# Causal maxima masked by halves of the keys, and a new order for the launch of a six-layer kernel

## The chip, the cores and the metric

One core of one Trainium2 chip. The metric is the device time in microseconds of one execution; the kernel before takes 808.35 us as the median of three runs.

## The reference, cut to what matters

Six residual layers on x of shape (4, 512, 128), each on the layer-normalised x. The change touches the first, a causal self-attention with 16 heads of 8 dimensions and rotary positions:

```
q = rope(xn @ wq + bq);  k = rope(xn @ wk + bk);  v = xn @ wv + bv
score = where(causal, q k^T / sqrt(8), -inf);  attn = softmax(score)
x = x + (attn v) @ wo + bo
```

Behind it come a cross-attention with 77 keys, a mixture of 8 experts of which each token takes 2, another self-attention, a single-head cross-attention and a convolutional feed-forward layer.

## The kernel before

Instructions are written for each engine in an order of its own, and semaphores tie them together. The 512 tokens of each of the 4 batches lie as 4 tiles of 128 partitions. An attention layer is cut into 16 units: unit g works on batch g // 4 and on 4 of the 16 heads. A0 is the causal layer, X0 the cross-attention, A1 the second self-attention. The units of A0 and X0 are one stream, those of A1 another.

**Maxima.** The softmax takes the true maximum of each row, so a unit computes its scores twice. First with queries as output partitions (`max_pe`, L574), from which VectorE reduces the negated maximum along the keys (`max_dve`, L590); GpSimd splits it in two bf16 parts (`neg_of`), TensorE turns them (`turn_pe`, L611) and a DMA puts them as further rows into the unit's stack. Then with keys as output partitions (`scores_pe`, L690), from which ScalarE takes the exponential (L715), GpSimd masks the diagonal block (L723) and TensorE multiplies with the values (`pv_pe`, L738). Each head's operands are split into bf16 parts, stacked along 64 rows, so two heads lie side by side in the array as rows 0 to 63 and 64 to 127 and can run at once. The maxima of a unit are 12 items, each one bank of up to 512 columns, with 16 diagonal blocks in all. To a diagonal block two more matmuls add -1e30 above the diagonal (`pair_q` with `behind_pair`, L578, and `even_q` with `behind_even`, L579), each with 64 rows, 128 weight columns and 128 streamed columns. Units 0 and 1 have their maxima ahead of the stream; those of unit g + 2 run between the scores of unit g.

**Launch.** Before unit 0 each batch goes through these steps. VectorE takes the moments of its rows (`moments_dve`, L450), GpSimd the inverse root (`norm_pool`, L477), VectorE normalises (L471), TensorE transposes (`norm_pe`, L528), ScalarE copies to `xnT` (`norm_act`, L542). TensorE projects q, q with neighbours swapped, k, k swapped, and v (`stage0_pe`, L1233 and L1236). VectorE adds the bias and multiplies with cosine and sine (`stage0_dve`, L1244 and L1247), GpSimd adds the two products (`roped_pool`, L1261), ScalarE rounds to the first bf16 part (`stage0_act`, L1275), VectorE subtracts it (`rest0_dve`, L1255), ScalarE rounds the second part (L1280), GpSimd subtracts again for the third (`part3_pool`, L1267). The parts lie in one buffer, `parts`. SP sends them to a stack in DRAM with six DMAs per batch (`stack_dma`, L914, three for q and three for k), and loads each unit's slot from there (`load_sp`, L638 and L644). GpSimd adds the output bias to x for each batch (`bias_pool`, L823).

The order by hand: all of GpSimd's constants come first, and TensorE and VectorE wait for all of them (`s_const`, 5). TensorE then takes the transposes of batches 0 and 1, the projections of 0 and 1, transposes of 2, projections of 2, transposes of 3, projections of 3, the 12 maxima of unit 0, its turn, the 12 maxima of unit 1, and unit 0. It and VectorE wait for all weights of the layer at once. ScalarE may write `parts` of a batch only when the stack DMAs of the batch before have landed. SP issues x of batch 0, ten loads, x of batches 1 to 3, the fills, further weights, the stack of batch 0, four slot loads, and the stacks of 1, 2 and 3, with the shift of unit 0's maxima ahead of the last.

Of the kernel before, what the change touches and what calls it, by code (L numbers as in the profile page):

```python
# [12 lines left out]
BF16 = mybir.dt.bfloat16  # L13
# [3 lines left out]
P = 128  # L17
NB, S, D = 4, 512, 128
QT = S // P
# [42 lines left out]
SLOT_DMAS = 2  # L62
TURNS = 4
# [181 lines left out]
def stacked_by(a, b, z):  # L245

    if z == 0:
        return 16 * RUNS * (NB * a.order + b + 1)
    return 16 * RUNS * (b + 1 if a is A0 else NB + 1 if a is X0 else NB + 2 + b)


def build(nc, d, out):
# [4 lines left out]
    with es:  # L257
# [12 lines left out]
        s["emptied"] = [sem(f"emptied{i}") for i in range(TURNS)]  # L270
        s["slot"] = [sem(f"slot{i}") for i in range(UNITS)]
# [17 lines left out]
        pair_q, even_q = sb("pair_q", [P, 2 * P], BF16), sb("even_q", [P, 2 * P], BF16)  # L289
        behind_pair, behind_even = sb("behind_pair", [P, 2 * P], BF16), sb("behind_even", [P, 2 * P], BF16)  # L290
# [91 lines left out]

        after_w = w12[:, 4:W_PIECES].rearrange("p a n -> p (a n)")
# [22 lines left out]
        s_x0, s_x = sem("s_x0"), sem("s_x")  # L406
        s_w, s_out_w, s_soon, s_later, s_experts = [sem(f"s_{n}") for n in ("w", "out_w", "soon", "later", "experts")]
        s_padded, s_padb = sem("s_padded"), sem("s_padb")
        s_fill, s_filled0, s_filled = sem("s_fill"), sem("s_filled0"), sem("s_filled")
        s_const = sem("s_const")  # L410
# [29 lines left out]
        def moments_dve(e, ln, b):  # L440

            n = norm_number(ln, b)
            if ln == 0:
                e.wait_ge(s_x0 if b == 0 else s_x, 16)
            else:
                e.wait_ge(*x_at[(ln - 1, b)])
# [110 lines left out]
        def half(t, j):  # L557
            return t[rows_of(j), P * j:P * (j + 1)]

        def max_pe(e, g, m):  # L560
# [7 lines left out]
            for qt in tiles:  # L568
                for h in hs:
# [58 lines left out]
        def load_sp(e, g):  # L628
# [4 lines left out]
            e.wait_ge(s["stacked_q"], stacked_by(a, b, 0))  # L633
            e.wait_ge(s["stacked_k"], stacked_by(a, b, 1))
# [246 lines left out]

        def split_pool(e, a, b, z, step):
# [3 lines left out]
            if step == 0:  # L886
                e.wait_ge(*emptied(("qk"[z], a.ln, b)))
                e.wait_ge(s["stacked_k" if z else "stacked_q"],
                          stacked_by(a, b, z) - 16 * RUNS)
# [11 lines left out]

        def stack_dma(e, a, b, z):
# [7 lines left out]
            for first, rows, part, same in (K_RUNS if z else Q_RUNS):  # L910
                src = parts[:, z, part:part + (1 if same else rows), 0:n]
# [357 lines left out]
        def stage0_act(e, b):  # L1269
# [6 lines left out]
            if b in (1, 2):  # L1276
                norm_act(e, 0, b + 1)
# [1120 lines left out]
```

## Time and profile before

| | |
|---|---|
| median of 3 runs | 808.35 us (808.21 to 808.52) |
| the profiled execution | 808.57 us, span 806.8 us |
| busy in the span | TensorE 652.0 us (81%), VectorE 568.1 (70%), ScalarE 431.9 (54%), GpSimd 285.3 (35%) |
| mean granted TensorE clock | 0.905 of 2.4 GHz |
| first score of unit 0 | 73.58 us |

The span runs from the first to the last instruction; what the run takes beyond it lies around the profiled instructions. In the rows below PE is TensorE, PEld its weight loads, DVE VectorE, ACT ScalarE, POOL GpSimd and SP the queue that issues most DMAs; PEclk is the granted clock of TensorE as a share of 2.4 GHz. A busy share says how full an engine is; the chain of work that ended last says which waits set the end.

### The profile page before, as it was taken

Reading aid. Unit: us, or ns where it says so; the run is one execution under the profiler, and the core shown is the slowest. Engines: PE = TensorE matmul, PEld = TensorE weight load, DVE = VectorE, ACT = ScalarE, POOL = GpSimd, SP = SyncE. Lnnn points to the kernel's source line nnn. Section 1 sums busy time; section 2 is a strip of 40 time slices with the busy share of each in tenths; the row PEclk is TensorE's granted clock in tenths of the full one; section 3 lists DMA queues with packets and bytes.
Section 4 is the critical chain, followed back from the end, with each engine's and each line's share of the span. In section 5 each row is a group of like instructions: output and inputs, shape, how many; then the busy total and the mean of one; then the engine's idle time right before and its main releaser. Section 6 shows DMA issues by size and latency. Waiting matters only on the chain.

```text
span 806.8 us, 16037 instructions
## 1 busy us (share of the span) xinstructions
PE 652.0 (81%) x5011; PEld 354.7 (44%) x5011; DVE 568.1 (70%) x1685; ACT 431.9 (54%) x825; POOL 285.3 (35%) x517
## 2 busy tenths in 40 slices
PE   2758999999978886169999924598899989997987
PEld 1334455444434443159999812132232323334543
DVE  3757678787757776737777626888898898943564
ACT  1322555666666543035566412086787777884544
POOL 5742444454551345713333301215132241341310
PEclk9885999999999999579999956598999999999999
DMA  7452655354223311211111135201322111000000
GB/s 221 149 199 83 199 163 171 113 176 145 71 67 99 102 53 63 77 32 51 52 48 48 42 108 182 78 27 34 127 81 78 54 29 52 2 2 1 13 14 27
DMA packets 72788, 67.18 MB, mean 83 GB/s; under 512 B 14545, under 2 KB 67217, under 8 KB 72705
## 3 DMA queue, kind: packets, MB, share of 16 engines
q1 hardware_dynamic: 70000, 60.68, 24.6%
q0 software_dynamic: 2272, 4.69, 1.8%
q8 instruction: 42, 0.69, 0.4%
q10 hardware_dynamic: 432, 0.79, 0.3%
q14 instruction: 42, 0.34, 0.1%
HBM read 37.74 MB, written 28.00 MB: 81 GB/s over the span
## 4 chain that ended last, share of the span: by engine, by line
PE 60%; DVE 20%; issue 7%; POOL 5%; ACT 4%; DMA 3%; SPq 1%; DVEq 0%; ACTq 0%; POOLq 0%
PE bank_pv L738 11%; DVE mx L590 11%; PE bank_turn L574 7%; PE bank_scores L2034 5%; PE bank_turn L1768 4%; PE bank_scores L1776 4%; PE bank_scores L1768 4%; PE bank_scores L690 4%; POOL routed_tokens L1732 2%; PE bank_turn L757 2%; DVE stats L450 2%; DVE xn L471 2%; PE bank_turn L799 2%; PE bank_turn L578 2%; PE bank_turn L528 2%
## 5 line engine op out<-in xcount | busy, mean ns | idle before, releaser
L590 DVE TENSOR_REDUCE mx<-bank_turn 128x1 f32<-128x512 f32 (+3 forms) x452 | 259.6, 615 | 60.3 <-PE bank_turn L579 31.4
L574 PE MATMUL bank_turn<-stk 64*128 64x77 bf16 (+4 forms) x708 | 160.1, 303 | 30.0 <-DVE mx L590 20.0
L690 PE MATMUL bank_scores<-stk 64*128 64x512 bf16 (+3 forms) x576 | 169.4, 355 | 4.8 <-ACT probs L711 3.6
L715 ACT ACTIVATE probs<-bank_scores 128x1024 f32<-128x1024 f32 (+4 forms) x160 | 117.2, 768 | 98.6 <-PE bank_scores L690 98.3
L711 ACT ACTIVATE probs<-bank_scores 128x512 f32<-128x512 f32 x256 | 138.6, 606 | 35.6 <-PE bank_scores L690 34.6
L738 PE MATMUL bank_pv<-probs,vsl 128*32 128x512 f32 (+3 forms) x1152 | 137.6, 550 | 2.8 <-POOL probs L723 1.8
L574 PEld LDWEIGHTS bank_turn<-stk 64*128 64x128 bf16 x708 | 52.2, 96 | 133.8 <-DVE mx L590 64.5
L723 POOL TENSOR_SCALAR_AFFINE_SELECT probs<-probs 128x256 f32<-128x256 f32 x128 | 51.8, 408 | 73.6 <-ACT probs L715 72.2
L1748 POOL DMA_INDIRECT expert_outputs<-probs,y_at x39 | 37.3, 957 | 83.2 <-DVE y_at L1645 78.8
L477 POOL TENSOR_TENSOR rstd<-var,mhalf 128x4 f32<-128x4 f32 x24 | 25.4, 1056 | 108.4 <-DVE var L456 108.2
L690 PEld LDWEIGHTS bank_scores<-stk 64*128 64x128 bf16 x576 | 45.6, 93 | 29.4 <-ACT probs L711 17.5
L528 PE MATMUL bank_turn<-ident,xn 128*128 128x128 f32 x60 | 13.0, 354 | 56.2 <-DVE xn L471 56.0
L579 PE MATMUL bank_turn<-behind_even,even_q 64*128 64x128 bf16 x256 | 53.1, 229 | 0.0
L578 PE MATMUL bank_turn<-behind_pair,pair_q 64*128 64x128 bf16 x256 | 53.0, 229 | 0.0
L2034 PE MATMUL bank_scores<-f_w1c,w 128*128 128x512 f32 x96 | 47.5, 634 | 0.4 <-ACT w L537 0.4
L604 POOL CAST neg<-mx 128x16 bf16<-128x16 f32 x33 | 6.5, 196 | 112.6 <-DVE mx L590 99.4
L590 DVE TENSOR_REDUCE mx<-bank_scores 128x1 f32<-128x512 f32 x60 | 40.8, 680 | 3.0 <-PE bank_scores L574 3.0
L1776 PE MATMUL bank_scores<-w,oT 128*128 x312 | 41.4, 276 | 1.3 <-DVE probs L1665 1.0
L1768 PE MATMUL bank_turn<-probs,w_now 128*128 128x128 f32 x320 | 42.2, 280 | 0.0
L542 ACT COPY xnT<-bank_turn 128x512 f32<-128x512 f32 x19 | 11.1, 583 | 55.8 <-PE bank_turn L528 55.8
L1768 PEld LDWEIGHTS bank_turn<-probs,w_now 128*128 128x128 f32 x320 | 40.1, 197 | 0.0
L1768 PE MATMUL bank_scores<-probs,w_now 128*128 128x128 f32 x304 | 39.1, 275 | 0.0
(303 smaller groups left out, 1163.0 us busy)
## 6 DMA issues: line engine op xcount, KB each, us to landing
stk<-stack_A SPq DMA_DIRECT2D x64, 256.0 KB, 3.1
w<-in_M_w SPq DMA_DIRECT2D x12, 512.0 KB, 4.8
stack_A<-parts SPq DMA_DIRECT2D x15, 384.0 KB, 3.2
stack_A<-fill SPq DMA_DIRECT2D x8, 512.0 KB, 5.3
stk<-stack_X SPq DMA_DIRECT2D x16, 256.0 KB, 2.7
stack_A<-parts SPq DMA_DIRECT2D x15, 256.0 KB, 3.2
probs<-routed_tokens SPq DMA_DIRECT2D x39, 65.0 KB, 1.9
w<-expert_outputs SPq DMA_DIRECT2D x4, 512.0 KB, 5.7
```

The lines of the kernel that those rows point to most:

```text
L574: mm = e.matmul(o, stk[r, slot, 0, pp, qt * P:(qt + 1) * P], stk[r, slot, 1, pp, 0:keys], start=True, stop=not a.causal)
L578: e.matmul(o, half(pair_q, j), half(behind_pair, j), start=False, stop=False)
L579: mm = e.matmul(o, half(even_q, j), half(behind_even, j), start=False, stop=True)
L590: e.tensor_reduce(o.rearrange("p h q -> p q h"), bank_of((g, m))[:, 0:k * keys].rearrange("p (q h k) -> p q h k", q=len(tiles), h=len(hs)) ...
L690: mm = e.matmul(score_bank(g, kt, i)[:, 0:S - q0], stk[r, slot, 1, pp, kt * P:(kt + 1) * P], stk[r, slot, 0, pp, q0:S], start=True, stop=True)
L711: e.activation(probs[:, probs_of(g, kt), j + 2 * pp], score_bank(g, kt, i), ACT.Exp, scale=1 / math.sqrt(HD)).then_inc(s["probs"], 1)
L715: e.activation(probs[0:a.kp, probs_of(g, kt), j:HG:2, 0:n], bank_scores[0:a.kp, 2 * j:2 * j + 2, 0:n], ACT.Exp, scale=1 / math.sqrt(HD)).t ...
L723: e.affine_select(out=o, in_=o, compare_op=ALU.is_ge, fill=0.0, base=0, pattern=[[0, 2], [1, P]], channel_multiplier=-1).then_inc(s["maske ...
L738: mm = e.matmul(bank_pv[VW * h:VW * (h + 1), q0:S], vsl[:, slot, kt, h, :], probs[:, probs_of(g, kt), h, 0:S - q0], start=(kt == 0), stop= ...
L1768: mm = e.matmul(hid[t % 2][z][:, c * P:(c + 1) * P], w_now[:, t % 2, o:o + P], x_inT[:, t % 2], start=True, stop=True)
L1776: mm = e.matmul(y_bank[:, 0:D], act[:, t % 2, c * P:(c + 1) * P], w2[:, bass.ds(ex[t], 1), c, :].rearrange("p o n -> p (o n)"), start=(c = ...
L2034: e.matmul(bank, f_xT[:, b, j * P + tap:j * P + tap + P], f_w1c[:, tap], start=(tap == 0), stop=False)
```

## The change

It has two parts.

**Masks by halves.** The four mask operands become two: `later_key` (256 columns, ones where the column is at most 63 behind the partition) and `masked_key` (a diagonal of -1e30). A diagonal block still takes two mask matmuls, but each covers 64 keys of the block: it streams 64 columns of `masked_key` against 128 weight columns of `later_key`.

**The launch order.** VectorE no longer waits for the constants before its first moments, TensorE waits for the identity alone, and GpSimd writes the constants that are wanted later behind the first inverse root. Weights have semaphores by q, k and v. x of batch 1 is loaded on ScalarE's queue. Batch b + 1 is transposed between the third and the fourth projection of batch b. The parts get two buffers by turns, `parts0`; the second lies in the last two pieces of the expert weights' buffer, whose loads wait for the stack DMAs of batch 3. Stack semaphores are counted by buffer. Projections of batch 3 stand between the first six and the last six maxima of unit 0. SP loads units 0 and 1 behind the stack of batch 0, units 2 and 3 behind that of batch 1. GpSimd adds the output biases of all four batches behind `neg` of unit 0.

```diff
+        def later_keys(j, k):
+            at = HR * (j + 1 - k)
+            return later_key[rows_of(j), at:at + P]
+        def masked_keys(j):
+            return masked_key[rows_of(j), HR * j:HR * (j + 1)]
...
                     if a.causal:
-                        o = o[:, qt * P:(qt + 1) * P]
-                        e.matmul(o, half(pair_q, j), half(behind_pair, j), start=False, stop=False)
-                        mm = e.matmul(o, half(even_q, j), half(behind_even, j), start=False, stop=True)
+                        for k in range(2):
+                            mm = e.matmul(o[:, qt * P + HR * k:qt * P + HR * (k + 1)], later_keys(j, k), masked_keys(j),
+                                          start=False, stop=k == 1)
...
+        late_w = w12[:, W_PIECES - 2:W_PIECES].rearrange("p a n -> p (a n)").bitcast(BF16)
+        parts0 = [parts, late_w[:, 0:6 * S].rearrange("p (z r n) -> p z r n", z=2, r=3)]
...
         def stage0_pe(e, b):
             x, w = turned_x(e, 0, b), wts["A0"]
             for i, t in enumerate((w["wq"], wsw[0], w["wk"], wsw[1])):
+                if b == 0 and i % 2 == 0:
+                    e.wait_ge(s_wk if i else s_wq, 16 * len(k_loads if i else q_loads))
                 wait(e, s["up_dve"], 4 * (b - 1) + i + 1)
                 e.matmul(up_banks[i], t[:], x, start=True, stop=True).then_inc(s["up_in"], 1)
+                if i == 2 and b + 1 < NB:
+                    norm_pe(e, 0, b + 1)
...
+        def stage0_act(e, b):
             for z in range(2):
+                e.wait_ge(s["roped"], 2 * b + z + 1)
+                parts_free(e, A0, b, z)
+                e.copy(parts0[b % 2][:, z, 0], roped(z)).then_inc(s["part1"], 1)
+                if z == 0 and b + 1 < NB:
+                    norm_act(e, 0, b + 1)
+                e.wait_ge(s["rest"], 2 * b + z + 1)
+                e.copy(parts0[b % 2][:, z, 1], rest[:, z]).then_inc(s["part2"], 1)
             e.wait_ge(s["up_in"], 5 * (b + 1))
             e.copy(vraw[:, QT * b:QT * (b + 1)].rearrange("p q d -> p (q d)"), bank_pv[:]).then_inc(s["up_act"], 1)
...
         def first_stream_pe(e):
+            e.wait_ge(s_ident, 2)
             norm_pe(e, 0, 0)
+            for b in range(NB - 1):
+                stage0_pe(e, b)
+            e.wait_ge(s_const, CONSTS)
+            for k in range(AHEAD):
+                max_pe(e, 0, k)
             stage0_pe(e, 3)
-            all_maxima_pe(e, 0)
+            for k in range(AHEAD, len(A0.items)):
+                max_pe(e, 0, k)
             turn_pe(e, 0)
             all_maxima_pe(e, 1)
...
             moments_dve(e, 0, 1)
             normalise(e, 0, 1)
+            for b in range(NB - 1):
+                stage0_dve(e, b, 0)
+                if b + 2 < NB:
+                    moments_dve(e, 0, b + 2)
+                stage0_dve(e, b, 1)
+                rest0_dve(e, b, 0)
+                if b + 2 < NB:
+                    normalise(e, 0, b + 2)
+                if b < NB - 2:
+                    rest0_dve(e, b, 1)
+            e.wait_ge(s_const, CONSTS)
             for k in range(len(A0.items)):
                 max_dve(e, 0, k)
+                if k == 1:
+                    rest0_dve(e, 2, 1)
+                if k == AHEAD - 1:
+                    for z in range(2):
+                        stage0_dve(e, 3, z)
+                if k in (AHEAD + 1, AHEAD + 3):
+                    rest0_dve(e, 3, (k - AHEAD) // 2)
...
             for b in range(NB):
+                roped_pool(e, b, 0)
                 if b + 2 < NB:
                     norm_pool(e, 0, b + 2)
+                roped_pool(e, b, 1)
+                for z in range(2):
+                    part3_pool(e, b, z)
+            values_pool(e, 0)
+            neg_of(e, 0)
+            for b in range(NB):
                 bias_pool(e, A0, b)
             neg_of(e, 1)
...
                 if b == 0:
                     e.wait_ge(s_filled0, 16 * len(fills_of(A0)))
-                    for g in range(UNITS):
+                if b < 2:
+                    for g in range(2 * b, 2 * b + 2):
                         load_sp(e, g)
...
         def weights_sp(e, n):
+            if n >= W_PIECES - 2:
+                for z in range(2):
+                    e.wait_ge(*stacked(A0, NB - 1, z))
...
         def _(e):
             e.memset(f_cb[:], 0.0).then_inc(s_padb, 1)
-            e.wait_ge(s_const, 5)
             first_stream_dve(e)
```

## Rows read from the trace of the kernel before

**Rows 1.** Busy time by stretch: start:end, length, engines, clock, DMA share, GB/s

```profile
0.00:73.40 73.40, 40.56 (x177) 22.48 (x178) 44.08 (x109) 15.22 (x25) 37.92 (x58) 0.82 0.56 178
73.40:216.00 142.60, 136.23 (x1454) 70.44 (x1453) 107.63 (x240) 84.36 (x132) 67.10 (x172) 0.96 0.47 145
```

**Rows 2.** Chain that ended last, 0 to 73.4 us: start, us, what

```profile
3.72 3.47 issue
...
14.25 2.63 DVE xn L471 x4
...
29.73 1.25 POOL x_sb L823
...
42.47 5.94 DMA stack_A<-parts
...
49.64 5.55 PE bank_scores L1233 x8
```

**Rows 3.** Timeline of the launch: start, us, engine, line, idle before and releaser

```profile
12.22 0.58 ACT L542 COPY xnT<-bank_turn 128x512 f32<-128x512 f32 x1 [10.14 <-PE bank_turn L528]
...
17.83 1.91 PE L1233 MATMUL bank_scores<-xnT,A_wq 128*128 128x512 f32 x2
...
25.95 1.40 DVE L1255 TENSOR_TENSOR rest<-probs,parts 128x512 f32<-128x512 f32 x2
...
28.68 3.67 SPq L914 DMA_DIRECT2D stack_A<-parts  x6
...
34.85 0.37 SPq L638 DMA_DIRECT2D stk<-stack_A  x1
...
46.55 0.62 ACT L1275 CAST parts<-probs 128x512 bf16<-128x512 f32 x1 [3.50 <-DMA stack_A<-parts]
...
56.55 0.42 DVE L590 TENSOR_REDUCE mx<-bank_turn 128x2 f32<-128x256 f32 x1 [0.58 <-PE bank_turn L579]
...
66.16 0.29 PE L611 MATMUL bank_turn<-identb,neg 128*32 128x128 bf16 x1 [1.45 <-POOL neg L606]
...
73.58 0.60 PE L690 MATMUL bank_scores<-stk 64*128 64x512 bf16 x1
```

**Rows 4.** VectorE's groups by shape, 0 to 73.4 us: busy, mean ns, idle

```profile
L471 DVE TENSOR_SCALAR xn<-x_sb,mv,rstd 128x128 f32<-128x128 f32 x16 | 9.6, 769 | 2.3 <-POOL rstd L477 2.3
...
L450 DVE BATCH_NORM_STATS2 stats<-x_sb 128x6 f32<-128x128 f32 x16 | 3.5, 280 | 6.7 <-issue 6.0 <-DVE xn L471 0.7
L1247 DVE SCALAR_TENSOR_TENSOR probs<-bank_scores,A_bk_swapped,cos_sin 128x512 f32<-128x512 f32 x4 | 3.0, 749 | 0.3
```

**Rows 5.** GpSimd's groups, 0 to 73.4 us

```profile
L1261 POOL TENSOR_TENSOR probs<-probs 128x512 f32<-128x512 f32 x8 | 10.1, 1270 | 8.9 <-DVE probs L1247 8.9
L1267 POOL TENSOR_TENSOR parts<-rest,parts 128x512 bf16<-128x512 f32 x8 | 9.1, 1152 | 10.3 <-ACT parts L1280 10.3
```

**Rows 6.** DMA issues, 0 to 75 us: count, KB each, median us to landing

```profile
stk<-stack_A SPq DMA_DIRECT2D x8, 256.0 KB, 4.5
```

**Rows 7.** Busy time by stretch, columns as in rows 1

```profile
55.00:82.00 27.00, 22.37 (x174) 12.98 (x172) 19.36 (x38) 7.00 (x11) 7.78 (x13) 0.62 0.28 96
```

**Rows 8.** Timeline of TensorE in a unit: two mask matmuls

```profile
115.66 0.22 PE L578 MATMUL bank_turn<-behind_pair,pair_q 64*128 64x128 bf16 x1
115.71 0.22 PE L579 MATMUL bank_turn<-behind_even,even_q 64*128 64x128 bf16 x1
```

**Rows 9.** Timeline of TensorE: maxima of X0, 77 columns streamed

```profile
222.25 0.20 PE L574 MATMUL bank_turn<-stk 64*128 64x77 bf16 x1
...
222.29 0.30 PE L574 MATMUL bank_turn<-stk 64*128 64x77 bf16 x4
...
222.43 0.27 PE L574 MATMUL bank_turn<-stk 64*128 64x77 bf16 x3
```

**Rows 10.** Chain that ended last, 73.4 to 216 us, by line

```profile
by line: PE bank_pv L738 23.7%; PE bank_turn L574 18.8%; PE bank_scores L690 11.0%; PE bank_turn L578 7.5%; DVE mx L590 7.3%; PE bank_turn L579 7.0%; PE bank_turn L757 5.4%; issue 2.8%; PE bank_turn L799 2.8%; PE bank_turn L841 1.8%; PE ban
```

**Rows 11.** Waits, 73.4 to 216 us: total, times, longest

```profile
DVE mx L590 <- PE bank_turn L579: 28.1, 51, 1.8
```

More of the change, by code:

```diff
@@ L62 @@
 SLOT_DMAS = 2
+CONSTS = 3
 TURNS = 4
@@ L270, in build @@
         s["emptied"] = [sem(f"emptied{i}") for i in range(TURNS)]
+        s["stacked0"] = [[sem(f"stacked0_{i}{n}") for n in "qk"] for i in range(2)]
         s["slot"] = [sem(f"slot{i}") for i in range(UNITS)]
@@ L910, in stack_dma @@
             for first, rows, part, same in (K_RUNS if z else Q_RUNS):
-                src = parts[:, z, part:part + (1 if same else rows), 0:n]
+                src = parts_of(a, b)[:, z, part:part + (1 if same else rows), 0:n]
                 if same and rows > 1:
                     src = src.to_broadcast([P, rows, n])
-                e.dma_start(to[:, first:first + rows, :], src).then_inc(s["stacked_k" if z else "stacked_q"], 16)
+                e.dma_start(to[:, first:first + rows, :], src).then_inc(stacked(a, b, z)[0], 16)
         def beside_pe(e, g, place, part):
@@ L1250, in rest0_dve @@
-        def rest0_dve(e, b):
-            for z in range(2):
-                n = 2 * b + z
-                e.wait_ge(s["part1"], n + 1)
-                wait(e, s["part3"], n - 1)
-                e.tensor_tensor(rest[:, z], roped(z), parts[:, z, 0], ALU.subtract).then_inc(s["rest"], 1)
-        def roped_pool(e, b):
-            for z in range(2):
-                e.wait_ge(s["up_dve"], 4 * b + 2 * z + 2)
-                wait(e, s["rest"], 2 * (b - 1) + z + 1)
-                e.tensor_tensor(roped(z), probs[:, 0, z], probs[:, 0, 2 + z], ALU.add).then_inc(s["roped"], 1)
@@ L1263, in part3_pool, with stage0_dve @@
-        def part3_pool(e, b):
-            for z in range(2):
-                e.wait_ge(s["part2"], 2 * b + z + 1)
-                wait(e, s["stacked_k" if z else "stacked_q"], 16 * RUNS * b)
-                e.tensor_tensor(parts[:, z, 2], rest[:, z], parts[:, z, 1], ALU.subtract).then_inc(s["part3"], 1)
-        def stage0_act(e, b):
+        def stage0_dve(e, b, z):
+            if b == 0:
+                e.wait_ge(s_wk if z else s_wq, 16 * len(k_loads if z else q_loads))
+            e.wait_ge(s["up_in"], 5 * b + 2 * z + 1)
+            wait(e, s["roped"], 2 * (b - 1) + z + 1)
+            e.scalar_tensor_tensor(probs[:, 0, z], up_banks[2 * z], wts["A0"]["bk" if z else "bq"][:], cos_sin[:, 0],
+                                   ALU.add, ALU.mult).then_inc(s["up_dve"], 1)
+            e.wait_ge(s["up_in"], 5 * b + 2 * z + 2)
+            e.scalar_tensor_tensor(probs[:, 0, 2 + z], up_banks[2 * z + 1], bsw[z][:], cos_sin[:, 1],
+                                   ALU.add, ALU.mult).then_inc(s["up_dve"], 1)
@@ new lines, in rest0_dve, with roped_pool @@
+        def rest0_dve(e, b, z):
+            n = 2 * b + z
+            e.wait_ge(s["part1"], n + 1)
+            wait(e, s["part3"], n - 1)
+            e.tensor_tensor(rest[:, z], roped(z), parts0[b % 2][:, z, 0], ALU.subtract).then_inc(s["rest"], 1)
+        def roped_pool(e, b, z):
+            e.wait_ge(s["up_dve"], 4 * b + 2 * z + 2)
+            wait(e, s["rest"], 2 * (b - 1) + z + 1)
+            e.tensor_tensor(roped(z), probs[:, 0, z], probs[:, 0, 2 + z], ALU.add).then_inc(s["roped"], 1)
```

168 lines of the change are left out of this document (68 added, 100 removed).

## The prediction

> **What bounds the kernel now.** I read the page first for its split of the span, then busy time by stretch, then the chain of work that ended last for the two stretches which the diff touches, and last the timeline around its steps. The launch runs from the start to unit 0's first score at 73.4 us; the sixteen causal units of A0 run from there to 216 us. In the launch no engine is full: VectorE, the busiest, works 44.1 of 73.4 us, TensorE 40.6 [rows 1]. In the units TensorE works 136.2 of 142.6 us [rows 1] and is the bound; no other stage holds an edited step but the two weight loads that may wait. So the launch is a matter of waits, the units a matter of TensorE's work, and the two add up, since every later stage hangs on the end of the units and not on a fixed moment.
>
> The chain of the launch shows four waits [rows 2]. VectorE's first statistics start 3.5 us after the tokens landed: they wait for the last constant. The projections of batch 0 wait behind the transposes of batch 1, whose normalisation takes 2.6 us; batch 0's own `xnT` is there at 12.8 us, its first projection starts at 17.8 [rows 3]. Later the chain leaves the engines: the stack DMAs of batch 1, from 42.5 on, land for 5.9 us, and only then may ScalarE write `parts` again (its cast waits 3.5 us for that DMA, at 46.55 [rows 3]), take `xnT` of batch 3 behind it, and let TensorE start batch 3's projections at 49.6 [rows 2]. The maxima stand behind these in TensorE's order: VectorE's first one starts at 56.55 us [rows 3], though unit 0's stack was loaded long before.
>
> **The launch, step by step.** The first wait goes: tokens are there at 3.7 us, so VectorE starts 3.5 us earlier. GpSimd still writes constants at that time, but the ones ahead of its first `pow` are a short list; I add 0.5 us for the others beside batch 0's normalisation. `xnT` of batch 0 then stands at 12.8 - 3.5 + 0.5 = 9.8 us, and its projections no longer queue behind batch 1: 9.8 for 17.8, a gain of 8.0. The batch's stack DMAs move with them, from 28.7 [rows 3] to about 20.7.
>
> From there the batches are paced by VectorE and no longer by `parts`, which now has two buffers: batch 2 waits for batch 0's DMAs, a batch earlier than before. VectorE's work for a batch is four bias-and-rotate steps of 0.75 us, a normalisation of 9.6/4 = 2.4, moments whose statistics take 3.5/4 = 0.9 [rows 4], with the aggregation about 1.5 (my estimate), and two `rest` of 0.70 [rows 3]: 8.3 in all, of which the last batches have less. GpSimd's share is two rotated sums of 1.27, two third parts of 1.15 [rows 5] and one `pow`, some 6 us, so it stays under VectorE. Batch 0's second `rest` ends at 25.95 + 1.40 = 27.35 us now [rows 3]; 8.0 earlier is 19.3, and with the transposes of batch 1 and the longer normalisation now within this batch I put it at 21. Batch 1 then ends at 29, and batch 2's four steps at 32. Slot 0 comes in time: six issues from 20.7 take till about 25 us, as they took 3.7 at 28.7 [rows 3], landing about 3 (before, from 32.35 to the first load at 34.85, 2.5), and the load 4.5 [rows 6], together 32.5. So the first maximum starts near 33.5 us, 23 earlier than at 56.55.
>
> Part of that is paid back. Batch 3's projections now stand between the two halves of unit 0's maxima. On VectorE that adds four steps of 0.75 (3.0 us; its two `rest` were between the maxima before too) and the time until TensorE has its first projection out, 1.9 [the pair in rows 3]: 5 us. `neg` of unit 0 now comes after batch 3's third part in GpSimd's queue, which I cost at 1.4 (one part and a cast behind the last `rest`). The four bias additions of 1.25 [rows 2], moved behind `neg` of unit 0, are 5.0 us on GpSimd beside the maxima of unit 1, which take from the turn at 66.2 to 73.4, 7.2 us [rows 3]: hidden; without that cover they would delay the turn of unit 1 by what is over. The other moves cost nothing on the path: x of batch 1 on ScalarE's queue stands ahead of work that waits for TensorE anyway, two loads of unit 2 and 3 now go out behind batch 1's stack on SP but are wanted only after unit 1's maxima, and the last two weight pieces wait for DMAs that are over ten units earlier. Should SP fall behind there, unit 2's maxima are late next, and those run inside unit 0.
> Sum for the launch: 23 - 5 - 1.4 = 16.6 us, unit 0 at 56.8 us.
> Bounds: if VectorE never idled after 3.7 us, its 44.1 us would end at 47.8, a gain of 25.6; it idles 29.3 now, and at least a few us remain by the waits through four engines: 21. At the low end TensorE runs batch 3's projections and the second half at the lower of its two clocks (0.62 granted from 55 to 82 us [rows 7]), which I bound by the first pair's 1.9 us against about 1.0, four pairs: 3.6, and slot 0 comes 2 late: 11.
>
> **The masks, step by step.** The count stays: two mask matmuls on each diagonal block, 512 in all. Each streams 64 columns instead of 128. The weight load of 128 columns stays. Today one mask starts 0.05 us after the other [rows 8]: the unit of its cost is 128 columns at the full clock, 53 to 55 ns. The trace has no mask of 64 columns; the nearest row is the maxima of X0, which load the same 64x128 weights and stream 77: eight in a row from 222.25 end at 222.70, each 0.20 long, so they follow each other by (0.45 - 0.20)/7 = 36 ns [rows 9]. So 64 columns cost at most 36 ns, and 64/128 of 55 = 28 at least. On the chain of the units the two mask lines hold 7.5 + 7.0 = 14.5% [rows 10], or 20.7 us of 142.6. A mask at 36 ns gives back 35%, at 28 ns 49%: 7.2 to 10.1. VectorE is the next to bind: it waits 28.1 us for L579 in this stretch [rows 11], so it has room, but some banks will then come free late, and a mask that ran beside a score gives back only what the score leaves. I take 7.0, near the lower end. Bounds: 2, if most of it goes to VectorE's reductions, and 10.5.
>
> The Trainium skill, in "TensorE: Matmul & The Clock Gate", section "Back-to-back issue gap", holds that in a stream of weight loads and matmuls the spacing is set by both, about 81 ns at 128 columns, and the section on LDWEIGHTS that a load takes by its own columns (128/1.2 = 107 ns) whatever is streamed. By these rules the halves would save nothing and the sum would be the launch alone, 16.6. The trace disagrees: 36 ns with 128-column weights [rows 9].
>
> **Sum.** The profiled execution took 808.57 us, 806.8 of them the span and 1.8 around it; the median of the runs is 808.35, 0.2 lower. 808.6 - 16.6 - 7.0 = 785.0, and against the median the same within what I can tell. A difference under 0.2% (1.6 us) is no change for this measurement.
>
> **Rivals.**
> 1. The masks give nothing, because the two loads of a pair, or VectorE's banks, set the pace: 808.6 - 16.6 = 792. For it speaks that TensorE already waits for banks in these units and that VectorE is busy 107.6 of 142.6 us [rows 1]; against it the 36 ns. The Trainium skill's two rules above, if they held here, would give this time. It decides if masks follow each other by more than 50 ns, or VectorE's wait for L579 goes under 10 us.
> 2. The launch keeps half: VectorE, which takes its orders strictly in turn, sits at the first maximum waiting for slot 0 with batch 2's `rest` and all of batch 3 behind it. Should slot 0 land 8 us later than I put it (batch 1's stack DMAs sharing the queues), the launch gains 8.6 and the time is 808.6 - 8.6 - 7 = 793. Against it: the DMAs of batch 1 are issued behind loads 0 and 1.
> 3. Slower: TensorE stays at the lower clock through the units. Its activity is what falls with shorter masks. The place is the stretch from 73.4 to 216, now at 0.96 granted [rows 1]; at 0.50 its 136 us of work could grow by as much again, and it turns the sign once the lower clock holds for about 47 us more (half of that is the gain of 23.6). At 820 it would hold for some 70. Against it: the units stay full of matmuls, and the stretch is at 0.96 already with TensorE as busy as it would be after.
>
> **How the numbers follow.** Both parts pay: 0.76, and 785 is its time, 777 to 793 its own range (21 + 10.5 = 31.5 gained at best; 11 + 4 = 15 at worst). Rival 1: 0.10, at 789 to 797. Rival 2: 0.09, at 790 to 800. Rival 3: 0.04, 810 to 830. A launch that gains nothing and masks that gain little: 0.01. The range takes the bounds of the first case, 11 + 2 at the low end and a little for VectorE's idle at the other: 775 to 797. Faster by over 0.2%: 0.95; within: 0.01; slower: 0.04.
>
> **What would show it.** Right: VectorE's first statistics near 3.8 us; first projection near 10; the chain without the stack DMAs of 5.9 us; first score of unit 0 near 57; mask matmuls 28 to 36 ns apart; the sixteen units in about 135 us for 142.6, TensorE still nearly full. Wrong: a wait of VectorE for a slot's load at 30 us; a granted clock near 0.5 past 70 us; VectorE's idle for L579 gone while the units take as long as before.

## The result, and the profile after

The kernel after takes 794.94 us as the median of four runs (790.39 to 797.58), the one before beside it 808.28. The ratio is 0.9833, with a 95% interval of 0.9805 to 0.9861: faster by 13.3 us where 23.6 were forecast, at 794.9 where 785.0 was forecast. That is inside the whole range of 775 to 797, but outside the 777 to 793 that the prediction gave its main case; the times of its rivals 1 and 2 cover it. The profiled execution is the fastest of the four, 790.39 us with a span of 788.6, so the rows below belong to a faster execution than the median.

Busy time of the kernel after by stretch (start:end, length, PE, PEld, DVE, ACT, POOL, granted clock, DMA share, GB/s). The first two answer to [rows 1]; the others are shorter stretches on which the text below rests. The record of the granted clock starts at 15.6 us, so 1.00 for what lies ahead says nothing.

```profile
0.00:59.40 59.40, 36.92 (x179) 20.02 (x180) 44.71 (x109) 14.95 (x25) 36.06 (x53) 0.86 0.68 220
59.40:200.50 141.10, 132.53 (x1455) 67.17 (x1454) 107.89 (x241) 84.20 (x133) 67.15 (x172) 0.94 0.47 146
4.78:33.25 28.47, 19.83 (x70) 10.17 (x70) 25.75 (x76) 7.47 (x13) 19.53 (x27) 1.00 0.75 233
33.25:52.79 19.54, 10.84 (x60) 5.95 (x59) 13.03 (x21) 6.20 (x11) 9.50 (x12) 0.75 0.60 213
118.00:121.00 3.00, 2.06 (x33) 1.01 (x28) 2.92 (x15) 2.16 (x3) 1.38 (x6) 1.00 0.71 214
121.00:125.00 4.00, 3.70 (x27) 1.34 (x25) 2.46 (x6) 1.88 (x3) 2.05 (x4) 0.57 0.17 31
39.00:42.00 3.00, 3.00 (x7) 1.36 (x6) 1.69 (x3) 0.07 (x1) 0.81 (x1) 0.50 1.08 378
```

The launch is 14 us shorter and VectorE works as long in it as before (44.7 us for 44.1): waits went, not work. The stretch of the units holds the same instructions (1455 on TensorE for 1454), and it is only 1.5 us shorter, 141.1 for 142.6. So the launch paid and the masks hardly seem to. (The prediction calls this stretch the sixteen units. It ends near the last mask in both kernels, and the scores of units 14 and 15 run behind it, so it holds fourteen.)

Timeline of the launch after, which answers to [rows 3]:

```profile
4.78 0.29 DVE L455 BATCH_NORM_STATS2 stats<-x_sb 128x6 f32<-128x128 f32 x1 [3.58 <-issue]
...
10.53 2.07 PE L1262 MATMUL bank_scores<-xnT,A_wq 128*128 128x512 f32 x2 [0.68 <-ACT xnT L547]
...
20.97 4.41 SPq L941 DMA_DIRECT2D stack_A<-parts  x6
...
21.46 0.68 DVE L1288 TENSOR_TENSOR rest<-probs,parts 128x512 f32<-128x512 f32 x1
...
29.94 0.68 DVE L1288 TENSOR_TENSOR rest<-probs,w 128x512 f32<-128x512 f32 x1
...
32.52 0.73 DVE L1281 SCALAR_TENSOR_TENSOR probs<-bank_scores,A_bk_swapped,cos_sin 128x512 f32<-128x512 f32 x1
...
32.90 0.23 PE L584 MATMUL bank_turn<-stk 64*128 64x128 bf16 x1
...
34.42 1.09 DVE L1288 TENSOR_TENSOR rest<-probs,parts 128x512 f32<-128x512 f32 x1 [1.16 <-ACT parts L1304]
35.43 0.41 DVE L600 TENSOR_REDUCE mx<-bank_turn 128x2 f32<-128x256 f32 x1
...
39.24 2.07 PE L1262 MATMUL bank_scores<-xnT,A_wq 128*128 128x512 f32 x2
41.10 1.91 PE L1262 MATMUL bank_scores<-xnT,A_wq_swapped 128*128 128x512 f32 x2
...
52.79 0.29 PE L621 MATMUL bank_turn<-identb,neg 128*32 128x128 bf16 x1 [4.07 <-POOL neg L616]
...
59.43 0.60 PE L700 MATMUL bank_scores<-stk 64*128 64x512 bf16 x1
```

Read it against the forecast: statistics at 4.78 us (3.8 forecast), first projection at 10.53 (9.8), stack DMAs at 20.97 (20.7), the batches' second `rest` over at 22.1 and 30.6 (21 and 29), batch 2's last step over at 33.25 (32). TensorE issues the first maxima at 32.9 without a wait, so slot 0 was there by then (32.5 forecast). But VectorE stands before them in a `rest` of batch 2 that waits 1.16 us for ScalarE's cast, which in turn waited for GpSimd's rotated sum, and its first maximum starts at 35.43 (33.5). Batch 3's first projections take about 2 us a pair at a granted clock of 0.50.

In the chain of the launch no step is a stack DMA any more. In the chain of the stretch of the units, by line:

```profile
by line: PE bank_pv L748 22.5%; DVE mx L600 17.5%; PE bank_turn L584 16.2%; PE bank_scores L700 10.6%; PE bank_turn L588 7.2%; PE bank_turn L767 5.8%; issue 3.3%; PE bank_turn L809 2.8%; PE bank_turn L851 1.8%; DVE xn L476 1.7%; ACT probs L
```

The masks (now L588) fell from 14.5% [rows 10] to 7.2%, from 20.7 to 10.2 us; VectorE's reductions (L600) rose from 7.3% to 17.5%, to 24.7 us. The masks themselves did what the change says. A piece of TensorE's timeline inside the units, and the waits of the stretch (what waited, for what: us in total, times, longest):

```profile
151.07 0.28 PE L584 MATMUL bank_turn<-stk 64*128 64x256 bf16 x1
151.19 0.22 PE L588 MATMUL bank_turn<-masked_key,later_key 64*128 64x64 bf16 x2
151.23 0.39 PE L700 MATMUL bank_scores<-stk 64*128 64x512 bf16 x1
```

```profile
DVE mx L600 <- PE bank_turn L588: 27.2, 46, 2.1
...
PEld bank_turn L584 <- DVE mx L600: 9.7, 28, 1.2
...
PE bank_turn L584 <- DVE mx L600: 4.7, 9, 0.9
```

One mask is 0.19 us long and a pair takes 0.22, so the second starts 0.03 us behind the first, for 0.05 before [rows 8]. The Trainium skill, "TensorE: Matmul & The Clock Gate", section "Back-to-back issue gap", has about 81 ns from one matmul to the next at 128 columns in a stream of weight loads and matmuls. The pairs here lie well under that, at 50 ns with 128 streamed columns and at 30 with 64; whether a long stream of them would, no run here shows. VectorE still waits 27.2 us for the masks, for 28.1 before [rows 11].

To compare the units between kernels I take two marks that hold the same work in each: ScalarE's copies of the outputs of unit 0 and unit 13 to `oT`. After:

```profile
72.16 0.59 ACT L760 COPY oT<-bank_pv 128x512 f32<-128x512 f32 x1
203.78 0.59 ACT L760 COPY oT<-bank_pv 128x512 f32<-128x512 f32 x1
```

131.62 us from one to the other, where the kernel before takes 132.85 (86.75 to 219.60). In the granted clock by single microseconds, the kernel after falls to 0.50 three times between these marks (near 85, 122 and 173 us), the one before once (near 99). Each fall lasts 3.4 us: between the marks the time at the lower clock is 10.2 us after and 3.4 before.

### The profile page after: what moved, and what is told of

Read it like the earlier page. It is cut to its first block, busy times and chain, and to the rows that moved or that the text cites. A ratio compares the mean times of both kernels' runs of the same rounds, so it can differ in the third digit from the quotient of the medians.

```text
span 788.6 us, 16027 instructions
## 1 busy us (share of the span) xinstructions
PE 642.6 (81%) x5006; PEld 348.9 (44%) x5011; DVE 568.7 (72%) x1685; ACT 431.5 (55%) x825; POOL 282.6 (36%) x512
## 4 chain that ended last, share of the span: by engine, by line
PE 56%; DVE 23%; issue 9%; POOL 5%; ACT 4%; DMA 2%; SPq 0%; DVEq 0%; POOLq 0%; ACTq 0%
DVE mx L600 12%; PE bank_pv L748 10%; PE bank_turn L584 7%; PE bank_scores L2069 5%; PE bank_turn L1803 5%; PE bank_scores L1803 4%; PE bank_scores L1811 4%; PE bank_scores L700 4%; POOL routed_tokens L1767 2%; PE bank_turn L767 2%; DVE xn L476 2%; DVE stats L455 2%; PE bank_turn L588 1%; PE bank_turn L809 1%; PE bank_turn L533 1%
## 5 line engine op out<-in xcount | busy, mean ns | idle before, releaser
L600 DVE TENSOR_REDUCE mx<-bank_turn 128x1 f32<-128x512 f32 (+3 forms) x452 | 259.6, 615 | 54.6 <-PE bank_turn L588 28.9
L584 PE MATMUL bank_turn<-stk 64*128 64x77 bf16 (+4 forms) x708 | 155.6, 305 | 34.3 <-DVE mx L600 23.4
L700 PE MATMUL bank_scores<-stk 64*128 64x512 bf16 (+3 forms) x576 | 171.6, 360 | 4.9 <-ACT probs L721 3.6
L588 PE MATMUL bank_turn<-masked_key,later_key 64*128 64x64 bf16 x512 | 51.1, 200 | 0.0
L588 PEld LDWEIGHTS bank_turn<-masked_key,later_key 64*128 64x128 bf16 x512 | 45.7, 102 | 11.3 <-issue 2.9
L2069 PE MATMUL bank_scores<-f_w1c,w 128*128 128x512 f32 x96 | 45.8, 614 | 0.4 <-ACT w L542 0.4
L600 DVE TENSOR_REDUCE mx<-bank_scores 128x1 f32<-128x512 f32 x60 | 40.8, 680 | 3.1 <-PE bank_scores L584 3.1
L1811 PEld LDWEIGHTS bank_scores<-w,oT 128*128 128x128 f32 x312 | 38.0, 192 | 1.2 <-issue 1.2
```

The lines of the kernel that those rows point to most:

```text
L584: mm = e.matmul(o, stk[r, slot, 0, pp, qt * P:(qt + 1) * P], stk[r, slot, 1, pp, 0:keys], start=True, stop=not a.causal)
L588: mm = e.matmul(o[:, qt * P + HR * k:qt * P + HR * (k + 1)], later_keys(j, k), masked_keys(j), start=False, stop=k == 1)
L600: e.tensor_reduce(o.rearrange("p h q -> p q h"), bank_of((g, m))[:, 0:k * keys].rearrange("p (q h k) -> p q h k", q=len(tiles), h=len(hs)) ...
L700: mm = e.matmul(score_bank(g, kt, i)[:, 0:S - q0], stk[r, slot, 1, pp, kt * P:(kt + 1) * P], stk[r, slot, 0, pp, q0:S], start=True, stop=True)
L1811: mm = e.matmul(y_bank[:, 0:D], act[:, t % 2, c * P:(c + 1) * P], w2[:, bass.ds(ex[t], 1), c, :].rearrange("p o n -> p (o n)"), start=(c = ...
L2069: e.matmul(bank, f_xT[:, b, j * P + tap:j * P + tap + P], f_w1c[:, tap], start=(tap == 0), stop=False)
```

## The experiments

Twelve runs follow, the first of them the kernel after once more. The table has their medians with the ratio to the kernel before on the same chip, and marks from their profiled executions in us: first score of unit 0, time from unit 0's output to unit 13's, falls of the granted clock in that time, unit 13's output, and the first load of routed tokens in the expert layer, the last mark ahead of the layers that vary most.

| | median, ratio [interval] | first score | units 0 to 13 | falls | unit 13 | experts |
|---|---|---|---|---|---|---|
| before | 808.3 | 73.6 | 132.85 | 1 | 219.6 | 347.9 |
| after | 794.9, 0.9833 [0.9805, 0.9861] | 59.4 | 131.62 | 3 | 203.8 | 332.1 |
| e1_again | 790.2, 0.9794 [0.9763, 0.9825] | 59.2 | 131.61 | 3 | 203.6 | 331.8 |
| e2_wide | 797.5, 0.9867 [0.9835, 0.9899] | 60.3 | 132.79 | 1 | 207.3 | 335.4 |
| e3_halves | 802.0, 0.9931 [0.9906, 0.9956] | 72.3 | 130.27 | 2 | 214.7 | 344.6 |
| e4_nomask | 783.3, 0.9705 [0.9673, 0.9737] | 57.6 | 124.15 | 2 | 194.2 | 323.3 |
| e5_relief | 779.6, 0.9627 [0.9593, 0.9662] | 57.6 | 120.69 | 0 | 191.4 | 319.1 |
| e6_wide_relief | 787.8, 0.9763 [0.9720, 0.9806] | 58.8 | 127.28 | 1 | 197.2 | 325.4 |
| e7_single | 791.6, 0.9815 [0.9776, 0.9854] | 62.5 | 128.70 | 1 | 204.1 | 332.2 |
| e8_stage3 | 792.8, 0.9786 [0.9735, 0.9836] | 58.8 | 132.78 | 4 | 204.4 | 333.9 |
| e9_late | 797.2, 0.9886 [0.9852, 0.9920] | 64.6 | 128.73 | 1 | 206.4 | 334.9 |
| e10_mixed | 790.9, 0.9796 [0.9765, 0.9826] | 59.9 | 129.60 | 1 | 202.6 | 332.0 |
| e11_turned | 793.1, 0.9824 [0.9790, 0.9858] | 64.5 | 127.42 | 0 | 205.2 | 332.9 |
| e12_neg_mixed | 790.1, 0.9800 [0.9773, 0.9827] | 59.2 | 129.52 | 1 | 201.9 | 330.0 |

**e1_again**: the kernel after, once more.

> The changed kernel itself once more, for its spread and for a second trace. Its four times lie between 790.4 and 797.6 us, those of before between 807.8 and 808.5. If the spread is TensorE's granted clock in the units of A0 (one theory), the profiled execution shows its stretches at 0.5 in other places than the first trace (81 to 89, 120 to 126, 171 to 177 us), and a mean clock that goes with its time: near 0.908 at 790, near 0.896 at 797. If the spread is DMA or launch (the rival), the first score of unit 0 moves by several us from 59.4 with the clock unchanged.

Median 790.16 (789.27 to 793.58). The nine executions of this kernel reach from 789.3 to 797.6 us, so a total tells no difference of a few us. Its marks up to the experts repeat those of the first profile within 0.3 us, the three falls at the same places, so neither theory finds its sign. What varies lies later, in layers that no edit here touches: from the experts' mark to the end the profiled executions with the new order take 456.0 to 463.3 us, and from 470 us on they spend between 39.0 (e6) and 62.5 us (e2) at the lower clock. That this time makes the slow executions slow is likely, but no trace of one was kept. I therefore compare marks.

**e2_wide and e3_halves**: one part of the change each. e2 has the new launch order and masks that stream 128 columns; e3 is the kernel before with the masks by halves.

```diff
-  masked_key = sb("masked_key", [P, P], BF16)          # e2
+  masked_key = sb("masked_key", [P, 2 * P], BF16)
-  e.matmul(o[:, qt * P + HR * k:qt * P + HR * (k + 1)], later_keys(j, k), masked_keys(j),
+  e.matmul(o[:, qt * P:(qt + 1) * P], later_keys(j, k), masked_keys(j, k),
```

> The changed kernel with its launch order, and the same two mask matmuls per block, but each streams 128 columns again (64 of them zeros), so only the length of a mask is undone. If the halves pay as predicted, this is 7 us slower than the changed kernel: 800 to 802. If VectorE's reductions take what the masks give (theory 1), it is 1 to 2 us slower at most, with the units' chain at some 14% masks and 7% reductions as before. If shorter masks also cost granted clock (theory 2), it is the same or faster than the changed kernel, 788 to 795, its times closer together, and its units show fewer stretches at 0.5.

> The kernel before with its launch order and only the masks by halves; the two new operands are written by GpSimd in a gap of its queue after the old ones. Predicted part: 808.3 - 7 = 801. Theory 1 (VectorE takes it): 806 to 807. Theory 2 (the clock takes it back too): 807 to 811, with stretches at 0.5 inside the units that the kernel before does not have.

The order alone brings the first score from 73.6 to 60.3 (13.3 us) and unit 13 from 219.6 to 207.3 (12.3). The halves alone bring 1.3 and 4.9. Together they brought 14.2 and 15.8, so the two parts add up nearly (17.2 at unit 13), and both pay. The total says the same of the halves: 0.9931 and its interval stay under 1. By medians the halves bring 7.3 us (e2 to e1_again) and 5.8 (before to e3), close to the 7.0 forecast, but only 3.6 and 3.3 of that are there at the experts; the rest arises in layers without masks, so as far as the traces show, the match of the medians is luck.

e2 shows one fall for three, as the clock theory had it. But the units of e7, e9 and e11 below have the short masks too, and one fall or none, so short masks do not bring the falls by themselves.

**e4_nomask**: the kernel after without the mask matmuls; its maxima run over the later keys too.

```diff
-                    if a.causal:
+                    if False:
```

> The changed kernel without any mask matmul, so the maxima of A0 run over keys that are masked too. It takes another 10 us of mask time off TensorE's chain in the units. If TensorE's work sets the units, 785. If VectorE's reductions do (theory 1), 790 to 794: again only 1 to 3 us. If the clock does (theory 2), 793 to 800, with more stretches at 0.5.

Units 124.15 us with two falls. The chain between the marks by line, before and in e4:

```profile
by line: PE bank_pv L738 23.2%; PE bank_turn L574 18.3%; PE bank_scores L690 10.0%; DVE mx L590 7.9%; PE bank_turn L578 6.6%; PE bank_turn L579 6.4%; PE bank_turn L757 5.8%; issue 3.7%; PE bank_turn L799 3.0%; ACT probs L715 2.2%; PE bank_t
...
by line: DVE mx L600 21.7%; PE bank_pv L748 20.6%; PE bank_turn L584 14.7%; PE bank_scores L700 8.6%; PE bank_turn L767 7.1%; issue 5.0%; PE bank_turn L809 3.2%; ACT probs L725 3.2%; PE bank_turn L851 2.1%; DVE xn L476 1.9%; DVE otok L780 1
```

Between the marks the masks stood on the chain of the kernel after with 6.7%, 8.8 us; leaving them out brings 7.5, of which one fall is a part. The median of 783.3 is near the 785 that TensorE's work alone would give.

**e5_relief and e6_wide_relief**: VectorE reduces only the first half of the keys of the causal layer's maxima, in the kernel after (e5) and in e2 (e6); the maximum is then not over all keys.

```diff
   bank_of((g, m))[:, 0:k * keys].rearrange("p (q h k) -> p q h k", q=len(tiles),
-                            h=len(hs)),
+                            h=len(hs))[:, :, :, 0:keys // 2 if a is A0 else keys],
```

> The changed kernel with VectorE's reductions for the causal maxima over the first half of the keys alone, which leaves out half of each row. Theory 1 (VectorE takes what the masks give): the sixteen units shorten, from the end of unit 0 to the end of unit 14 by 6 us or more under the changed kernel's 131.6. Rival (TensorE still sets the units, and the clock alone took the rest): they shorten by under 3 us. Read by the ends of units, not by the total, since the later layers spread by several us from one execution to the next.

> The same half reductions with the masks streaming 128 columns again. With VectorE out of the way, theory 1 expects the full price of the mask length between this and the run with half reductions: 6 to 9 us from the end of unit 0 to the end of unit 14, against 1.2 us (132.8 to 131.6) with whole reductions. The rival expects the difference to stay at 1 to 3 us.

With VectorE relieved the units take 120.69 us, 10.9 less than after and, at an equal number of falls, 6.7 less than e11's 127.42. TensorE's instructions are the same, so VectorE does set part of the pace now. The chain of e5's units by line, from its first score to 188 us:

```profile
by line: PE bank_pv L748 26.3%; PE bank_turn L584 19.4%; PE bank_scores L700 13.0%; PE bank_turn L588 8.7%; PE bank_turn L767 5.9%; DVE mx L600 4.8%; PE bank_turn L809 3.1%; issue 2.4%; DVE xn L476 2.2%; PE bank_turn L621 2.0%; PE bank_turn
```

L600 is at 4.8% for 17.5%, and there is no fall of the clock. Between e6 and e5 the halves bring 6.6 us with one fall less, so some 5.2 without it, under the 6 to 9 that theory 1 expected.

**e7_single**: one buffer for the parts, as before.

```diff
-        parts0 = [parts, late_w[:, 0:6 * S].rearrange("p (z r n) -> p z r n", z=2, r=3)]
+        parts0 = [parts, parts]
...
-                wait(e, done, n - 16 * RUNS)
+                if b:
+                    e.wait_ge(*stacked(A0, b - 1, z))
```

> The changed kernel with one buffer for the parts again: a batch's parts wait for the stack DMAs of the batch before. If the second buffer is what lets the batches go at VectorE's pace, as the prediction had it, the first score of unit 0 moves from 59.4 to 66 us or more. If the order of the work alone does it (rival), it stays within 2 us of 59.4.

The first score comes at 62.5 us, 3.1 later, between what the two theories gave. The wait that the second buffer took away is back on ScalarE:

```profile
36.58 0.62 ACT L1305 CAST parts<-probs 128x512 bf16<-128x512 f32 x1 [4.95 <-DMA stack_A<-parts]
```

But of 4.95 us of waiting only 3.1 reach the first score, and nothing reaches the experts (332.2 for 332.1): the units have two falls less. The stack DMAs of 5.9 us which the prediction read in the chain were worth about half of their length.

**e8_stage3**: all of batch 3's projections and steps ahead of unit 0's maxima.

```diff
+            rest0_dve(e, 2, 1)
+            for z in range(2):
+                stage0_dve(e, 3, z)
             e.wait_ge(s_const, CONSTS)
             for k in range(len(A0.items)):
```

> The changed kernel with batch 3's projections ahead of all maxima of unit 0, in TensorE's order and VectorE's. In the changed kernel TensorE comes to them at the lower clock, after waiting at the first maxima, and they take 6.3 us. If that costs the 2 to 3 us that the launch lies behind its forecast of 56.8, the first score comes at 57 to 58 us here, with these projections at the full clock. If VectorE's order sets the time anyway, it stays at 59 to 60, and if the split of the maxima hides slot 0's load, it comes later, at 61.

The first score comes 0.7 us earlier than after, though VectorE's first maximum is 6.5 later (41.91). The same launch came at 59.2, 59.4 and 59.9 us in e1, after and e10, so 0.7 is hardly a difference. So batch 3 in the middle of the maxima buys nothing here; its projections run partly at the lower clock in this order too (1.69 and 1.91 us a pair at 35.2 and 36.7).

**e9_late and e11_turned**: two parts of the launch undone. In e9 VectorE's first statistics wait for the key weights; in e11 TensorE turns batch 1 ahead of batch 0's projections.

```diff
         def first_stream_dve(e):
+            e.wait_ge(s_wk, 16 * len(k_loads))          # e9
...
             norm_pe(e, 0, 0)
+            norm_pe(e, 0, 1)                            # e11, and not in stage0_pe(e, 0)
```

> The kernel after, in which VectorE waits for batch 0's key weights before its first statistics, so that these start near 7.7 us for 4.78. Theory (the launch is one chain through VectorE from its first statistics to unit 0's first score, which is what the prediction's 'if VectorE starts 3.5 earlier' says): first score 59.4 + 2.9 = 62.3, between 61.5 and 63. Rival (a later wait, for slot 0 or for batch 3's projections, takes up the delay): first score within 1 us of 59.4.

> The kernel after, in which TensorE turns batch 1 ahead of batch 0's projections, as before. Theory (the order of the two was worth the 5 us of the prediction's first projection that the earlier start does not explain): first projection near 14.7 us for 10.53, first score 59.4 + 4.2 = 63.6. Rival (VectorE normalises batch 1 ahead of batch 0's first bias step in any order, until 14.0 us, so that an early projection waits for it): the first bias step moves from 13.95 to about 15.8 us, and the first score by 2 at most, 59.4 to 61.4.

In e9 the statistics start at 9.22 us, 4.4 later (7.7 was expected), and the first score comes 5.2 later: no step of the launch has slack to take up a late start. The 0.7 us beyond it may be the clock: two pairs of batch 2's projections take 1.83 and 1.91 us in e9 for 1.02 after. In e11 the order costs as much:

```profile
13.89 1.11 PE L533 MATMUL bank_turn<-ident,xn 128*128 128x128 f32 x4 [4.23 <-DVE xn L476]
14.79 1.91 PE L1262 MATMUL bank_scores<-xnT,A_wq 128*128 128x512 f32 x2
```

TensorE sits 4.23 us before batch 1's transposes, the projection moves from 10.53 to 14.79 and the first score from 59.4 to 64.5, 5.1 us. The rival had VectorE busy until 14.0 in any case and at most 2 us lost; its first bias step moved by 2.9 (to 16.82), and the launch lost 5.1.

**e10_mixed and e12_neg_mixed**: in e10 the masks of units 6, 7, 11 and 12 stream 128 columns again; they run where the clock falls at 120 and 171 us. e12 adds `neg` of unit 0 ahead of batch 3's last third part.

```diff
+                            if g in (6, 7, 11, 12):
+                                mm = e.matmul(o[:, qt * P:(qt + 1) * P], later_keys(j, k), masked_keys(j, k),
...
+                if b == NB - 1:
+                    neg_of(e, 0)                        # e12
+                part3_pool(e, b, 1)
```

> The kernel after, in which the masks of units 6, 7, 11 and 12 stream 128 columns again; their maxima run where the granted clock falls at 120 and 171 us. Theory (shorter masks cost the clock there, because TensorE idles beside VectorE's moments of X0's batches): those two falls are gone, units 0 to 13 take 128 to 130 us for 131.6, and the start of the later part comes 2 us earlier. Rival (the falls have another cause, and the longer masks cost their length): the falls stay, the units take 132 to 133 us.

> As e10_mixed, and GpSimd makes neg of unit 0 ahead of the last third part of batch 3. Theory (the third part and the copy of values stand 0.85 us between VectorE's last maximum and neg): turn of unit 0 near 51.9 us for 52.79, first score near 58.6 for 59.4, and the median 0.8 under that of e10_mixed at the start of the later part. Rival (unit 1's maxima are held by VectorE or by something that does not move): first score 59.2 to 59.6.

In e10 the fall at 172 us is gone, the one at 122 stays, and the one at 85, among masks that were not changed, is gone too. The units take 129.60, 2.0 less. That is the size the theory gave but not its pattern, and 129.6 is near what one fall and four units of longer masks would give (128.7 and 1.2, the share of 4 of 14 units in the 4.1 below). So why the clock falls is not settled by it. The later start of e10's experts shows nothing (332.0 for 332.1). In e12 unit 0 is turned 0.71 us behind VectorE's last maximum (51.83 to 52.54) instead of 1.42, and the first score comes at 59.2 for e10's 59.9, which is no more than one launch varies by. No version that does all the work beats the kernel after by more than its executions differ: 790.05 (787.84 to 792.20) for e12.

**What the falls cost.** The kernels whose units are the same, masks of 64 columns and full reductions, differ in the falls alone: 127.42 us with none (e11), 128.70 and 128.73 with one (e7, e9), 130.27 with two (e3), 131.62 and 131.61 with three (after, e1), 132.78 with four (e8). That is 1.2 to 1.6 us a fall, 1.4 in what follows. One place shows it directly: e9 and e11 bring out the first eleven units within 0.02 us of each other, up to 175.6 us. There e9 has its one fall, and its next unit takes 12.00 us where e11's takes 10.69. With masks of 128 columns and one fall it is 132.85 and 132.79 (before, e2). So at an equal number of falls the halves bring 132.8 - 128.7 = 4.1 us between the marks, and after gives 2.9 of it back by two more falls.

The stretch of e11's units, and e2's, between their marks:

```profile
77.73:205.15 127.42, 118.36 (x1363) 60.74 (x1360) 101.31 (x237) 79.27 (x128) 64.60 (x164) 1.00 0.51 155
```

```profile
74.50:207.29 132.79, 125.99 (x1363) 64.86 (x1360) 101.48 (x237) 79.76 (x128) 64.62 (x164) 0.99 0.48 149
```

TensorE works 7.6 us less in e11 and idles 9.1 us for 6.8. So 2.3 us of its saving turn into idle time. Its waits for VectorE's reductions to free a bank grow about as much, from 11.2 us (7.9 of the weight loads and 3.3 of the matmuls) to 14.0 (9.3 and 4.7).

## Why the prediction was right, and where it was off

**The launch, 16.6 forecast, 13.3 by the order alone (e2), 14.2 with the shorter masks.** The mechanism held. The milestones up to batch 2 came within 1.6 us, and undoing single parts costs what the steps said: a late start moves the first score by at least its own length (e9), the order of the transposes is worth 5.1 us (e11; the prediction's 8.0 less the 3.0 of the start is 5.0), the second buffer 3.1 (e7). With the start, 7.2 to 4.8 us, these come to about 10.6 of the 13.3; of the other moves only the split of the maxima was tried alone, and it gave nothing (e8). Two terms were mis-sized. "The first maximum starts near 33.5 us": it started at 35.43, not for slot 0 but for a `rest` of batch 2, which the diff puts ahead of it and which waited for ScalarE and GpSimd. That VectorE paces the batches held up to batch 2's last step, with VectorE at work for 25.8 of 28.5 us, but not from there to the turn of unit 0, where it works 13.0 of 19.5 us and waits by turns for ScalarE and TensorE. And batch 3's payback from the first maximum to the turn was to be 9.6 + 5 + 1.4 = 16.0 and took 17.4, with the projections at the lower clock, which the prediction had in its low bound. Unit 1's maxima then took 6.6 us for 7.2. 1.9 + 1.4 - 0.6 is about the 2.6 us by which the first score came late (59.4 for 56.8).

**The masks, 7.0 forecast.** The spacing came as forecast, 30 ns. The sum failed at the step "on the chain of the units the two mask lines hold ... 20.7 us ... A mask at 36 ns gives back 35%". The share of the chain is not what the masks cost. At equal falls the units without any mask take 124.15 - 2 x 1.4 = 121.3 us, with halves 127.4, with whole masks 131.4: between the marks all masks cost 10.1 us, where they hold 6.6% and 6.4% of the chain before, together 17.3 us; and halving them gave 4.0, 40% of the 10.1. These are estimates, as they price every fall at 1.4.

Of what left the chain, much came back as VectorE's reductions: between the marks these hold 10.5 us before and 26.9 in e4. From e2 to e11 TensorE's work shrinks by 7.6, some 6.3 without the fall, and 2.3 of that turn into idle time, which leaves 4.0. With VectorE relieved the same comparison gives 127.28 - 1.4 - 120.69 = 5.2, so VectorE keeps at least 1.2 of it. Even there the masks leave the chain with 8.5 us (14.4% of 127.3 us in e6, 8.1% of 120.7 in e5), so their share is too high for another reason as well, which is not shown. Outside the marks, e2 and after show 0.8 in the launch and 1.5 in unit 0, before and e3 1.3 and 1.1, part of it at unlike clocks. In all, e2 to after is 3.5 us at unit 13 and 6.4 without the two more falls. That this is near 7.0 is part luck: 0.8 of it lies in the launch's 64 masks, which the forecast did not count.

**The sum.** At unit 13's output the kernel after is ahead by 15.8 us: 14.2 from the launch, 0.4 in unit 0 and 1.2 between the marks. 23.6 were forecast. Of the 7.8 missing, the order's 13.3 for 16.6 are 3.3; 1.1 more goes in unit 0 under the new order (first score to output 14.2 us in e2 for 13.2 before, with 9.4 us at the lower clock for 7.1); 2.9 are the two more falls, and 0.6 the masks. Behind that mark the profiled executions differ by some us in either direction (15.8 at the experts, 18.2 at the end of the span), and the medians by 13.3; how the gain ends at 13.3 in the median is not shown. Two signs of the prediction failed beside the total: the stretch of the units took 141.1 us where about 135 were to show it right, and a granted clock near 0.5 past 70 us, which was to show it wrong, came for 3.4 us at a time.

**The rivals.** The first (masks give nothing) names what limits them: VectorE's banks do take a part, but e3 is faster than before by itself. Its sign, VectorE's wait for the masks under 10 us, did not appear (27.2). The second gave nearly the measured median (793) by another way: VectorE did stand at the first maxima, but for batch 2's `rest`, and lost 2 us, not 8. The third was right in kind and small: TensorE's clock falls more often, three times for 3.4 us instead of once, and costs 2.9 us, not 35. The sum had put this term at nothing. Its reason, the shorter masks, is not borne out, since e11 has them and no fall.

**What stays open.** Why the falls come at these places. One follows a stretch in which VectorE's moments and normalisation leave TensorE partly idle (118 to 121 us, 2.06 of 3.00 busy, then 0.57 granted). But e11 passes the same work with TensorE no busier and keeps the full clock throughout:

```profile
123.00:126.00 3.00, 1.81 (x25) 0.88 (x24) 2.92 (x14) 2.32 (x3) 2.15 (x6) 1.00 0.48 155
```

So the idle time alone does not decide it. Nor do the units' work and its time since the start. Here is e9 ahead of its fall and in it, and e11 below in the same stretches; up to 175 us the engines are equally busy in both:

```profile
172.00:175.00 3.00, 2.29 (x34) 1.33 (x34) 2.95 (x6) 1.21 (x2) 2.69 (x7) 1.00 0.70 209
175.00:178.70 3.70, 3.70 (x26) 1.38 (x23) 1.93 (x4) 2.74 (x4) 1.53 (x4) 0.54 0.18 45
...
172.00:175.00 3.00, 2.28 (x34) 1.31 (x34) 2.97 (x6) 1.20 (x2) 2.68 (x7) 1.00 0.70 214
175.00:178.70 3.70, 3.64 (x37) 2.00 (x34) 2.16 (x5) 3.23 (x5) 1.54 (x4) 1.00 0.19 46
```

In the launch, VectorE starts only at 4.78 us for the forecast 3.8 because batch 0's tokens land later: issued at 0.80 us in both kernels, they take 3.9 us to land after and 2.9 before. That x of batch 1 now loads beside them on another queue is the likely reason, and it wasn't tried alone.

## What to carry to other kernels

A line's share of the chain is not what it costs, and where a second engine follows closely the price is far below it: between the marks 17.3 us on the chain, 10.1 us when the masks were left out. Price such a line by leaving it out. Where one engine paces a launch, a later first step (4.4 us) or another order of the work that serves that engine (4.3 us at the first projection) reached the end in full, while a wait of 5 us on another engine was worth 3. And compare two kernels at marks that hold the same work and at an equal number of clock falls, before a few us are put down to an edit.

## What the hardware showed beside this

The granted clock falls to 0.50 for 3.4 us at a time inside busy units, and one such fall costs 1.2 to 1.6 us: from none to four falls the same instructions took 127.4, 128.7, 130.3, 131.6 and 132.8 us. Their number follows neither the units' work nor its time: e9 and e11 run their units at the same times and have one and none; with none, e11 made up all but 0.8 of its 5.1 us by the experts. Two executions of one kernel had them at the same places within a microsecond, but in the later layers the profiled executions with the new order differed by up to 23 us of time at the lower clock (39.0 to 62.5 us).
